# Experts' up projection with W1 stationary and features on the partitions

## What is computed

```python
logits = x @ Wr + br
idx = jnp.argmax(logits, axis=-1)
probs = jax.nn.softmax(logits, axis=-1)
gates = jnp.take_along_axis(probs, idx[..., None], axis=-1)[..., 0]
for ei in range(e):
    h = jax.nn.gelu(xf @ W1[ei] + b1[ei], approximate=False)
    y = h @ W2[ei] + b2[ei]
    mask = (idxf == ei).astype(xf.dtype)
    out = out + y * (gf * mask)[:, None]
```

## Time and profile before

| | |
|---|---|
| median of 3 runs | 580.57 us (579.96 to 581.64) |
| profiled execution, first to last instruction (span) | 575.1 us |
| TensorE busy | 407.0 us, 71% |
| TensorE weight loads | 288.6 us, 50% |
| VectorE busy | 303.8 us, 53% |
| ScalarE busy | 176.3 us, 31% |
| GpSimd busy | 115.0 us, 20% |
| mean granted TensorE clock | 0.824 of full speed |

### The profile page before, as it was taken

One profiled execution on the slowest core, in us unless ns is written; L12 is line 12 of the kernel. 1 busy time (PEld: TensorE's weight loads), 2 busy tenths in 40 slices (PEclk: granted clock), 3 DMA queues, 4 the chain that ended last, 5 costly groups with the idle time before them and its releaser, 6 DMA issues. The chain is left out here.

```text
span 575.1 us, 7947 instructions
## 1 busy us (share of the span) xinstructions
PE 407.0 (71%) x2743; PEld 288.6 (50%) x2743; DVE 303.8 (53%) x820; ACT 176.3 (31%) x398; POOL 115.0 (20%) x130
## 2 busy tenths in 40 slices
PE   4525634948789789879778857816651299999995
PEld 3314424536566676666655736605431045656554
DVE  3783500775875966958958859537324011212121
ACT  2223122444453454453644613503011011111010
POOL 2966201300320221123013110100013201010101
PEclk9977857959969969799799896975565599999999
DMA  8454956554665472271551621198632401011100
GB/s 226 101 136 90 197 115 119 188 136 109 184 142 153 134 146 79 87 135 55 128 114 43 142 63 37 44 342 287 177 128 72 154 1 50 22 52 28 36 17 12
DMA packets 52953, 64.42 MB, mean 112 GB/s; under 512 B 12797, under 2 KB 45552, under 8 KB 52912
## 3 DMA queue, kind: packets, MB, share of 16 engines
q1 hardware_dynamic: 37916, 43.89, 31.9%
q10 hardware_dynamic: 13828, 17.23, 9.3%
q0 software_dynamic: 1168, 2.76, 1.5%
HBM read 49.40 MB, written 14.99 MB: 112 GB/s over the span
## 5 line engine op out<-in xcount | busy, mean ns | idle before, releaser
L569 PE MATMUL ps<-W 125*32 125x112 f32 (+2 forms) x1280 | 102.8, 290 | 33.0 <-DMA W<-d_nm 15.1
L569 PEld LDWEIGHTS ps<-W 125*32 125x32 f32 (+2 forms) x1280 | 71.5, 139 | 56.7 <-issue 17.0
L573 PE MATMUL ps<-idf,hold 128*128 128x128 f32 (+4 forms) x288 | 48.5, 296 | 60.2 <-DVE hold L1483 19.1
L569 PE MATMUL ps<-W,hold 128*128 x264 | 86.2, 470 | 4.4 <-DVE hold L1891 4.4
L1591 DVE TENSOR_REDUCE mx<-ps 112x1 f32<-112x375 f32 x128 | 61.5, 540 | 26.1 <-PE ps L569 25.8
L573 PEld LDWEIGHTS ps<-idf,hold 128*128 128x128 f32 (+4 forms) x288 | 36.6, 158 | 75.0 <-issue 27.9
L1012 ACT ACTIVATE hold<-ps 128x224 f32<-128x224 f32 (+4 forms) x80 | 33.1, 429 | 109.8 <-PE ps L573 76.8
L569 PEld LDWEIGHTS ps<-W,hold 128*128 128x128 f32 x264 | 47.9, 191 | 26.7 <-issue 22.7
L1161 ACT ACTIVATE W<-ps 125x448 f32<-125x448 f32 x96 | 44.9, 545 | 31.5 <-PE ps L569 31.5
L1374 POOL TENSOR_TENSOR rstd<-ve,expo 112x1 f32<-112x1 f32 x32 | 18.3, 573 | 136.2 <-DVE ve L1483 136.2
L1312 ACT ACTIVATE hold<-ps 128x512 f32<-128x512 f32 x22 | 13.1, 598 | 102.2 <-PE ps L569 102.2
(11 more groups left out here) (157 smaller groups left out, 596.9 us busy)
## 6 DMA issues: line engine op xcount, KB each, us to landing
W<-in_L_ffn_W ACTq DMA_DIRECT2D x16, 1024.0 KB, 9.7
hold<-in_ctx SPq DMA_DIRECT2D x16, 375.0 KB
d_k<-W SPq DMA_DIRECT2D x8, 562.5 KB, 4.4
W<-d_k SPq DMA_DIRECT2D x8, 562.5 KB
hold<-d_mask SPq DMA_DIRECT2D x8, 492.2 KB, 3.7
d_xs<-hold SPq DMA_DIRECT2D x1, 3598.0 KB, 21.6
hold<-d_xs SPq DMA_DIRECT2D x12, 257.0 KB, 2.7
W<-d_k SPq DMA_DIRECT2D x8, 375.0 KB
```

What stands on the lines that cost most here:

```text
L569: return pe.matmul(o, lhsT=l, rhs=r, start=start, stop=stop, skip_group_check=True)
L573: return pe.transpose(o, i, ident[0:n, 0:n])
```

## The change

The up projection of each block is turned round. The 128x128 pieces of W1 become stationary and the block's 128 tokens the moving columns, so that the result has features on the partitions: for each of eight pieces of 128 features, two fp32 matmuls over the halves of K write 128 columns. ScalarE applies the Gelu to each piece, with the bias b1 read per partition from a new tile b1T (a transposed copy of b1, an input of its own that the host lays out), and writes directly to hxT, what the down projection reads. The eight transposes (e_hT on TensorE), their two copies on VectorE, the tile hx and the two bias matmuls go.

A stationary operand lies in a fixed tile: VectorE copies the expert's W1, 128x2048, from late into one of two tiles w1st (e_stage), the second of which reuses the SBUF of the attention's projection weights, now carved from one tile proj. e_stage(0) and e_stage(1) stand behind the routing, ahead of e_xT(0), with a wait for all weights; e_stage(j + 2) stands ahead of e_xT(j + 2) in the loop. The biases that GpSimd splits shrink from 1280 to 256 columns (b2 alone), with the load of b1 to ebn gone from the head of ScalarE's queue, and the load of b1T added behind Wr's. h1_ps and gelu_done now count eight for each block.

```diff
-    FB = F1 + D
+    FB = D
-        WqT = sb("WqT", [128, DC, DC, 128])
-        WkT = sb("WkT", [128, DC, DC, 128])
-        WvT = sb("WvT", [128, DC, D])
-        WoT = sb("WoT", [128, DC, D])
+        proj = sb("proj", [128, DC * F1])
+        WqT, WkT = (proj[:, i * 512:(i + 1) * 512].rearrange("p (k m d) -> p k m d", k=DC, m=DC) for i in range(2))
+        WvT, WoT = (proj[:, i * 512:(i + 1) * 512].rearrange("p (k d) -> p k d", k=DC) for i in (2, 3))
+        b1T = sb("b1T", [128, NE * M1])
-        hx = hb(128, 2, F1)
+        w1st = [hb(128, DC * F1), proj[:, :]]
...
             def e_up(j):
-                e = expert(j)
                 pe.wait_ge(xT_sb, j + 1)
+                pe.wait_ge(w1_staged, j + 1)
                 if j >= 2:
-                    pe.wait_ge(gelu_done, 2 * (j - 1))
-                for n in range(F1 // 512):
-                    o = ps[:, 2 * (j % 2) + n, :]
-                    mm(o, selx[:, j, :], ebt[:, 512 * n:512 * n + 512], True, False)
+                    pe.wait_ge(gelu_done, M1 * (j - 1))
+                for f in range(M1):
+                    o = ps[:, 2 * (j % 2) + f // 4, 128 * (f % 4):128 * (f % 4) + 128]
                     for k in range(DC):
-                        last = mm(o, xsT[:, j % 2, k, :], late[:, bass.ds(e * EW + k * F1 + 512 * n, 512)], False, k == DC - 1)
+                        last = mm(o, w1st[j % 2][:, k * F1 + 128 * f:k * F1 + 128 * f + 128], xsT[:, j % 2, k, :], k == 0, k == DC - 1)
                     last.then_inc(h1_ps, 1)
...
-                mm(pO[:, 0:D], selx[:, j, :], ebt[:, F1:FB], True, False)
+                mm(pO[:, 0:D], selx[:, j, :], ebt, True, False)
                 for f in range(M1):
-                    if f % 4 == 0:
-                        pe.wait_ge(hT_sb, 2 * j + f // 4 + 1)
+                    pe.wait_ge(gelu_done, M1 * j + f + 1)
...
                 with filled_block(pe, total, j):
-                    e_hT(j)
                     e_down(j)
...
+            act.dma_start(b1T[:, :], A["L1_ffn_b1T"]).then_inc(b1_loaded, 16)
...
-                    for n in range(2):
-                        act.wait_ge(h1_ps, 2 * j + n + 1)
-                        if j >= 2:
-                            act.wait_ge(hT_ps, 2 * (j - 2) + n + 1)
-                        act.activation(hx[:, j % 2, 512 * n:512 * n + 512], ps[:, 2 * (j % 2) + n, :], ACT.Gelu)\
-                           .then_inc(gelu_done, 1)
+                    e = act.value_load(ebi[0:1, j:j + 1], min_val=0, max_val=NE - 1)
+                    if j >= 2:
+                        act.wait_ge(y_ps, j - 1)
+                    for f in range(M1):
+                        if f % 4 == 0:
+                            act.wait_ge(h1_ps, M1 * j + f + 4)
+                        act.activation(hxT[:, j % 2, f, :], ps[:, 2 * (j % 2) + f // 4, 128 * (f % 4):128 * (f % 4) + 128],
+                                       ACT.Gelu, bias=b1T[:, bass.ds(e * M1 + f, 1)]).then_inc(gelu_done, 1)
...
+            def e_stage(j):
+                e = dve.value_load(ebi[0:1, j:j + 1], min_val=0, max_val=NE - 1)
+                if j >= 2:
+                    dve.wait_ge(h1_ps, M1 * (j - 1))
+                dve.tensor_copy(w1st[j % 2], late[:, bass.ds(e * EW, DC * F1)]).then_inc(w1_staged, 1)
...
             dve.wait_ge(sel_ready, 1)
+            dve.wait_ge(w_loaded, 16 * 2 * NE)
+            dve.wait_ge(xn3_stored, 16 * B)
+            e_stage(0)
+            e_stage(1)
             e_xT(0)
             e_xT(1)
             total = blocks(dve)
             for j in range(NB):
                 if j + 2 < NB:
                     with filled_block(dve, total, j + 1):
+                        e_stage(j + 2)
                         e_xT(j + 2)
                 with filled_block(dve, total, j):
                     e_tokens(j)
-                    e_hT(j)
                     e_y(j)
```

More of the change, by code:

```diff
@@ L255, in pixart_block @@
         bias_loaded = sem("bias_loaded")
+        b1_loaded = sem("b1_loaded")
+        w1_staged = sem("w1_staged")
         qr_made = sem("qr_made")
@@ L295, in pixart_block @@
         h1_ps = sem("h1_ps")
-        hT_ps = sem("hT_ps")
-        hT_sb = sem("hT_sb")
         h_evac = sem("h_evac")
@@ L951, in e_up @@
             def e_up(j):
-                e = expert(j)
                 pe.wait_ge(xT_sb, j + 1)
+                pe.wait_ge(w1_staged, j + 1)
                 if j >= 2:
-                    pe.wait_ge(gelu_done, 2 * (j - 1))
-                for n in range(F1 // 512):
-                    o = ps[:, 2 * (j % 2) + n, :]
-                    mm(o, selx[:, j, :], ebt[:, 512 * n:512 * n + 512], True, False)
+                    pe.wait_ge(gelu_done, M1 * (j - 1))
+                for f in range(M1):
+                    o = ps[:, 2 * (j % 2) + f // 4, 128 * (f % 4):128 * (f % 4) + 128]
                     for k in range(DC):
-                        last = mm(o, xsT[:, j % 2, k, :], late[:, bass.ds(e * EW + k * F1 + 512 * n, 512)], False, k == DC - 1)
+                        last = mm(o, w1st[j % 2][:, k * F1 + 128 * f:k * F1 + 128 * f + 128], xsT[:, j % 2, k, :], k == 0, k == DC - 1)
                     last.then_inc(h1_ps, 1)
-            def e_hT(j):
-                for n in range(2):
[L967 to L973, removed]
             def e_down(j):
@@ L1018, in load_expert @@
                               A["L1_ffn_W2"][e].rearrange("(m p) d -> p m d", p=128)).then_inc(w_loaded, 16)
-            for i, (n, cols) in enumerate((("L1_ffn_b1", slice(0, F1)), ("L1_ffn_b2", slice(F1, FB)))):
-                act.dma_start(ebn[:, cols], A[n]).then_inc(eb_loaded, 16)
+            act.dma_start(ebn, A["L1_ffn_b2"]).then_inc(eb_loaded, 16)
             act.dma_start(brow[0:1, 0], A["L0_xcond_bq"].unsqueeze(0)).then_inc(bias_loaded, 16)
@@ L1304, in _ @@
             act.wait_ge(sel_ready, 1)
+            act.wait_ge(b1_loaded, 16)
             total = blocks(act)
@@ L1357, in w_eb @@
                     if n == 0:
-                        pool.wait_ge(eb_loaded, 32)
+                        pool.wait_ge(eb_loaded, 16)
                         pool.tensor_copy(eb3[:, 0, :], ebn).then_inc(eb_step, 1)
@@ L1875, in e_xT @@
                 if j >= 2:
-                    dve.wait_ge(h1_ps, 2 * (j - 1))
+                    dve.wait_ge(h1_ps, M1 * (j - 1))
                 dve.tensor_copy(xsT[:, j % 2], pC[:, 0:D].rearrange("p (k t) -> p k t", k=DC)).then_inc(xT_sb, 1)
+            def e_stage(j):
+                e = dve.value_load(ebi[0:1, j:j + 1], min_val=0, max_val=NE - 1)
+                if j >= 2:
+                    dve.wait_ge(h1_ps, M1 * (j - 1))
+                dve.tensor_copy(w1st[j % 2], late[:, bass.ds(e * EW, DC * F1)]).then_inc(w1_staged, 1)
             def e_tokens(j):
@@ L1883, in e_tokens @@
                 dve.tensor_copy(tid[:, j % 4:j % 4 + 1], rid[:, j % 4:j % 4 + 1])
[L1885 to L1892, removed]
             def e_y(j):
@@ L1917 @@
         'L0_xcond_bk', 'L0_xcond_Wv', 'L0_xcond_bv', 'L0_xcond_Wo', 'L0_xcond_bo', 'L0_ffn_w1', 'L0_ffn_conv_w',
-        'L0_ffn_conv_b', 'L0_ffn_w2', 'L1_xcond_W_a', 'L1_xcond_W_c', 'L1_ffn_W1', 'L1_ffn_b1', 'L1_ffn_W2', 'L1_ffn_b2',
+        'L0_ffn_conv_b', 'L0_ffn_w2', 'L1_xcond_W_a', 'L1_xcond_W_c', 'L1_ffn_W1', 'L1_ffn_W2', 'L1_ffn_b2',
         'L1_ffn_Wr', 'L1_ffn_br']
@@ L1933 @@
         aps[name] = nc.dram_tensor(f"in_{name}", a.shape, _mybir.dt.from_np(a.dtype), kind="ExternalInput").ap()
+    b1T = _np.ascontiguousarray(_np.asarray(inputs["L1_ffn_b1"]).reshape(8, 8, 128).transpose(2, 0, 1).reshape(128, 64))
+    arrays["in_L1_ffn_b1T"] = b1T
+    aps["L1_ffn_b1T"] = nc.dram_tensor("in_L1_ffn_b1T", b1T.shape, _mybir.dt.float32, kind="ExternalInput").ap()
     out = nc.dram_tensor("out_x", inputs["x"].shape, _mybir.dt.float32, kind="ExternalOutput").ap()
```

## The result

The changed kernel takes 552.72 us (median of 4 runs, 549.78 to 557.32) where the kernel before takes 580.27: ratio 0.9539, 95% interval 0.9477 to 0.9600, 27.6 us between the medians. The direction was forecast, the size was not: 559.4 was predicted, with a range from 555.0. The profiled execution of the changed kernel spans 552.8 us and took 554.58. Ratios and their intervals leave out executions more than 1.5% above the fastest of their kernel, to which the profiles of experiments 2, 4 and 8 belong; medians keep them.

The account below looks back on a forecast made before the run. The prediction took TensorE's matmuls to bound the experts' loop. Loop -21.6, scatter +1.7 and start -1.3 summed to -21.2 us, so span 575.1 became 553.9, and with 5.5 around it 559.4 us; range 555 to 565.

Parts of the forecast that it names:

- The loop: Experts' blocks on TensorE: period 9.88 to 7.86 us, 20.2 saved, plus 0.8 and 0.6 at the edges, 21.6 us in all.
- The spacing: Turned up projection: each fp32 instruction with 128 moving columns takes 0.110 us, 32 with the switch 3.62 us against 4.37.
- The 0.159: Up projection instruction by the skill page's 81 to 56 ns ratio, in us; a block would be 1.6 us dearer.
- the rival's 0.144: Up projection: weight loads not hidden, 0.144 us an instruction, 12.0 us dearer, 571.4 us; chance 0.08.
- Hidden work: In the loop, ScalarE's Gelus and VectorE's weight copy cost nothing; the copy has over 4 us of cover.
- their wait comes back: Loop: transposes go but TensorE waits for staged weights or Gelus instead, 14 us dearer, 573.7 us; chance 0.04.
- the clock, the rival on the slower side: Granted clock falls inside the experts' loop; a block at half clock takes 15.4 us, whole loop 641; chance 0.04.
- The scatter: Before the loop, two weight copies on VectorE slow GpSimd's scatters: 1.7 us lost, bounds 0 and 2.5.
- The start: GpSimd's smaller bias split frees SyncE's clearing earlier, less an added b1 load: 1.3 us saved, bounds -2.2 and +0.5.
- What lies around the span: Whole run: the median of 580.57 lies 5.5 us above the profiled span of 575.1, and this was kept unchanged.
- the sum of 21.2: Whole kernel: -21.6 in the experts' blocks, +1.7 at GpSimd's scatters, -1.3 at the beginning, 21.2 us saved.

Follow-up runs that it names:

- experiment 2: Changed kernel with b1 and b2 loaded and split together again, 1280 columns as before the change: 555.08 us, ratio 0.9578 to the kernel before.
- experiment 4: Changed kernel with VectorE's first two weight copies held back until all of GpSimd's scatters have landed: 552.18 us.
- Experiment 8: Changed kernel with the first two weight copies behind the scatters and the load of b1T moved behind the batches: 550.45 us, ratio 0.9514; again 547.02 us.
- Experiment 5: Kernel before without the two bias matmuls of each up projection, b1 left out: 563.32 us against 578.04, ratio 0.9773.
- experiment 6: Changed kernel with eight transposes of the identity put back ahead of each down projection, without waits or copies: 563.38 us.
- experiment 7: Changed kernel with each weight copy of the loop made four times, the first two blocks' once: 552.99 us.
- experiment 3: Kernel before with only b2 loaded and split, 256 columns, b1 left out: 577.53 us against 580.20, ratio 0.9954.

## Why the prediction was wrong

**The loop** is the step that failed: of the terms of the sum it was mis-sized most, 21.6 forecast, 23.2 between the two profiles (111.3 to 88.1), 22.8 to 24.5 over all of the table. The period gave 2.23 a block and not 2.02. The down projection came down from 3.65 to 3.55, probably because its first matmul no longer starts behind a wait; the prediction had kept it. The bias step is 0.21 and not 0.27, the up projection 3.57 and not 3.62. Over nine or ten periods that is 2 us too little. At the ends the last two combining steps lie 546.57 - 542.07 = 4.50 us apart for the 4.67 forecast, and the first up projection saved 0.4 and not 0.8 (464.36 - 458.48 = 5.88 us, at a mean granted clock of 0.60 where the one before had 0.68). That last number is not a steady one: in the other profiles the first up projection of the changed code takes 5.1 to 6.3 us.

**The spacing** of 0.110 us was right: 32 instructions start to start with the switch make 3.57 / 32 = 0.112. The 0.159 that the prediction estimated from the Trainium skill ("TensorE: Matmul & The Clock Gate", section "Back-to-back issue gap") does not show here, nor does the rival's 0.144; they would have asked for periods of about 9.4 and 8.9 us. But the prediction noted the going of the bias matmuls only in passing and gave it no price of its own. Experiment 5 shows that all of the up projection's gain, and more, is theirs. They cost 1.03 us a block. The turned product is 0.13 dearer; its part is that it allows the bias in the Gelu and spares the transposes, 0.87 (0.88 in experiment 6), and 0.46 at the down projection's bias, of which 0.40 is the wait. Together 1.03 - 0.13 + 0.87 + 0.46 = 2.23, the whole of what the period lost.

**Hidden work** was right. Weight copy and Gelus cost the loop nothing (experiment 7, and no wait for them in the chain). The rival "their wait comes back" did not happen, and the clock, the rival on the slower side, is 1.00 from 470 to 538 us.

**The scatter**: 1.7 forecast, 1.0 to 1.15 measured; the mechanism was the one named (experiment 4). The two copies followed each other closely, and nearly all of the loss fell on the one scatter at 443.28; 0.9 us for each was too much.

**Between the scatter and the loop** the prediction had no term. In the profiles of the kernel before the first up projection starts 1.64 to 1.67 us behind the transposes, and without the bias matmuls 1.78 (experiment 5), in the changed kernel 1.18 us (1.24 in experiment 7): 0.5 us saved, which is not the bias matmuls' going and whose cause stays open.

**The start**: 1.3 forecast; 2.0 in the two profiles, 1.6 and 2.7 us in the medians of experiments 2 and 3. The four steps shrink to 44.62 to 48.95, and SyncE no longer waits for them. By the table, the clearing starts 2.1 us earlier in the mean (55.29 in the three profiles before with the long split, 53.20 in the six of the changed kernel that keep the early load of b1T). Experiment 8 moves that load away: ScalarE's first copy begins at 19.17 and 19.54 where those six have 20.00 to 21.63, and the scores start at 76.87 and 77.20 where they have 77.04 to 79.54, 78.3 in the mean. That is about 1.3 us in the mean, more than the load's own issue of 0.49, though single profiles overlap.

**What lies around the span** was taken wrongly. "I let this stand for what lies around it" gave 580.57 - 575.1 = 5.5 us to that, where time less span is 1.8. As a point forecast this did no harm, since 559.4 is also the median less 21.2. It hid something: an execution of 576.9 beside a median of 580.57 means that one kernel differs from itself by several us, 13 in the widest set of runs, by the table most of it in the batches and up to 2.7 in the start. It also explains why the two profiles differ by 22.3 us and the medians by 27.6: the profiled execution was 3.4 us under the median of 580.3 before, and 1.9 over that of 552.7 after. That the sum of 21.2 came so near to 22.3 is luck: the batches happened to be 2.1 us longer in the second profile, which hid what the terms lacked. The range of 10 us was made of the bounds of the edits alone, with no room for this. The changed kernel's own median was 548.85, 552.72 and 553.52 in three sets of runs; all three are outside the range.

Put together: loop 23.2, start 2 to 2.7, the step into the loop 0.5, less scatter 1.1, make 24.6 to 25.3 us, which would be 555.0 to 555.7, at the lower edge of the range. So the mis-sized terms use up the room under the forecast, and do not by themselves carry the time out of it. The medians say 26.7 to 29.0, with intervals of 3 to 4 us on either side, and the sum lies within two of the three. What is left, 1.4 to 4.4 us, would have to lie in the batches if it is not noise; the profiles show no shortening there, and whether a shifted start changes how long the clock stays low in them stays open. Settling it would take many more profiles of each kernel.

## What to carry to other kernels

Ask of every profile whether it is a typical execution (its time is the span and about 1.8 us here, not the median), and how far the stages that the edit leaves alone wander from one execution to the next: a range narrower than that is wrong whatever the sum. Look at small matmuls of another type between long fp32 ones: two bias matmuls of 512 columns cost this loop 1 us in 9.9, so moving a bias to the activation, which this kernel does with features on the partitions, may be the larger part of such a change. VectorE copies beside GpSimd's indirect DMAs were free in a loop with slack, and cost 1 us for 2.6 us of copies where those DMAs are the chain: try placing them behind.

## What the runs showed of the hardware

- An fp32 matmul instruction with 128 columns moving and a new 128x128 stationary operand runs at 0.112 us start to start, in streams of 32, at a granted clock of 1.00. 256 columns take twice as long (3.55 / 16 = 0.22), so the time goes with the columns and no part of the weight load shows in it.
- Two bf16 bias matmuls with 24 rows and 512 columns, standing between fp32 products, cost 1.03 us.
- One VectorE copy of 128x2048 fp32 from SBUF to SBUF takes 1.227 us. An indirect DMA's issue on GpSimd went from 0.95 to 1.97 us at the scatters beside two such copies, and at the output from 0.97 to between 1.47 and 1.94 beside one and to between 1.99 and 2.17 beside four.
